# Limiting the chosen row numbers in four one-column instructions instead of one of four columns

## The chip, the cores and the metric

The kernel runs on one core of a Trainium2 chip. The metric is the time on the device in microseconds (us), as the median of a few runs. The engines are named as the profile names them: PE (TensorE's matmuls) and PEld (its weight loads), DVE (VectorE), ACT (ScalarE), POOL (GpSimd) and SP (SyncE, which issues most of the DMAs here).

## The reference, cut to what matters

```python
x = x + xattn(ctx, layernorm(x))      # x: 4 x 512 x 512, ctx: 4 x 512 x 128, "adj" is the normalized x
x = x + ffn(layernorm(x))             # 4 experts, token i goes to expert i % 4

# in each of the two attention layers, for 8 heads:
e = leaky_relu(attn_self[:, :, None] + attn_neigh[:, None, :], 0.2)
e = e + MASK_VAL * (1.0 - adj)[None, :, :]          # MASK_VAL = -1e10
alpha = softmax(e)
out = elu(alpha @ feat + b)

# in the ffn, for each expert:
inter = silu(gate) * up
out = inter @ down_proj
```

The mask is 1e10 times a normalized number, so that each row's softmax picks one row: the one at which x is largest. The attention becomes a table lookup. Row i of the attention's output is row f(f(i)) of a table y, where f(i) is the place of the largest number in row i of x. The kernel computes y for all rows, finds f, follows it twice, and adds the found row of y to x. A separate part counts in how many rows the pick is sure, and a general program is there for inputs where it isn't.

## The kernel before, in words

The four batches b have 512 rows each, laid out as 128 partitions by four tiles e (the tile is also the expert). All matmuls of the second attention layer and of the ffn are done in three terms on a high and a low part of each operand, and the low part is a subtraction on VectorE or on GpSimd, chosen by hand.

Each engine has its own list of steps, written out by hand, and the steps meet through semaphores. There are no planned times: a step runs when all before it on its engine have been issued and its semaphores have come. Of interest here:

- VectorE finds the row: `find_top(b, e)` (line 1252, the largest of each row), `find_row(b, e)` (line 1256, its place), and once per batch `rows(b)` (line 1260), which limits the places of the batch's four tiles to at most N - 1 and writes them to `f_row`. `rows(0)` to `rows(3)` stand in VectorE's list between the steps `y_value(n)` (line 1246, a tile of the table y), `h_value(b, c)` (1227), `h_low(b, c)` (1239), `r_low(r)` (1207), `turned_low(e, b)` (1286), `x2_stats` (1265), `x2_moments` (1269 and 1271) and `normalize(e, b)` (1278).
- SP stores: `store_y(n)` (line 668) puts a tile of y into the table in HBM, and `store_f(b)` (672) puts the row numbers of a batch there. Both stand in one queue with the loads of weights and inputs.
- GpSimd follows and gathers: `follow(b, e)` (line 808) fetches f(f(i)) with an indirect DMA, once `store_f(b)` has landed, and the third and fourth of a batch also wait for the first and second to have landed. `gather(b, e)` (820) adds the found rows of y to `x_sb` with an indirect DMA. Between them stand low parts, `h_low(b, c)` (801) and `r_low(r)` (795), and `x2_inverse(e, b)` (828), one over the square root of the variance.
- ScalarE makes the high parts, the exponentials and the seeds of the banks: `seed(n)` (959), `y_exp_of(n)` (965), `h_high` (950), `r_high(r)` (926), `turned_xn` (975).
- PE: `layer0`, `layer1_part` (line 1631), `turn_xn(e, b)` (1645), `first_gate` and `first_up` (1656), and then the experts (1695, 1709). Its list runs layer1_part(12, 0), layer1_part(12, 1), first_gate(0), layer1_part(12, 2) ... layer1(15), turn_xn(0, 1), first_up(0), first_gate(1), turn_xn(0, 2), first_up(1).

Of the kernel before, what the change touches and what calls it, by code (L numbers as in the profile page):

```python
# [25 lines left out]
ALU = mybir.AluOpType  # L26
# [350 lines left out]
def build(nc, x, ctx, W0, a_self0, a_neigh0, b0, W1, a_self1, a_neigh1, b1, gate_up, down, out,  # L377
          ctx_t, W0_t, W1_t, b0_t, b1_t, gate_up_t, down_t):
    B, N, D = x.shape
    F_IN = ctx.shape[2]  # L380
    H, _, FO = W0.shape
    E = gate_up.shape[0]
# [14 lines left out]
    with ExitStack() as stack:  # L397
        def sem(name):
            return stack.enter_context(nc.semaphore(name))
# [26 lines left out]
        found = sb("found", [P, B, E, 8], U32)  # L426
        f_row = sb("f_row", [P, B, E], U32)
# [127 lines left out]
        f_made = sem("f_made")  # L555
# [84 lines left out]
        def _(sp):  # L640
# [27 lines left out]
                sp.dma_start(y_rows[n // E][n % E], val[:, n % E, :]).then_inc(y_stored[n % E], 16)  # L668

            def store_f(b):  # L670
                sp.wait_ge(f_made, b + 1)
                sp.dma_start(f_rows[b], f_row[:, b, :]).then_inc(f_stored[b], 16)

            def store_out(e, b):
# [41 lines left out]
            load_r(6)  # L716
            store_y(1)
            store_f(0)
            store_y(2)
            load_r(4)  # L720
# [4 lines left out]
            store_y(4)  # L725
            store_y(5)
            store_f(1)
            store_y(6)
            store_y(7)
            store_y(8)  # L730
            store_y(9)
            store_f(2)
            store_y(10)
            store_y(11)
# [462 lines left out]
        def _(dve):  # L1197
# [59 lines left out]

            def rows(b):
                dve.wait_ge(row_found, E * (b + 1))
                nc.vector.tensor_scalar(f_row[:, b, :], found[:, b, :, 0], float(N - 1), None,  # L1260
                                        ALU.min).then_inc(f_made, 1)

            def x2_stats(e, b):
                dve.wait_ge(gathered[b][e % 2], 16 * (e // 2 + 1))
# [148 lines left out]
            find_row(0, 3)  # L1413
            y_value(1)
            rows(0)
            y_value(2)
            find_top(1, 0)
# [15 lines left out]
            h_low(2, 1)  # L1433
            h_low(2, 2)
            rows(1)
            y_value(6)
            r_low(3)
# [16 lines left out]
            find_row(2, 3)  # L1454
            h_value(3, 2)
            rows(2)
            find_row(3, 0)
            h_value(3, 3)
# [503 lines left out]
```

## Time and profile before

| | |
|---|---|
| median of 3 runs | 220.52 us (220.13 to 221.07) |
| the profiled execution | 221.49 us |
| its span in the trace | 219.7 us |
| granted clock of PE | 0.997 of full |
| PE busy | 204.8 us, 93% |
| DVE busy | 153.9 us, 70% |
| ACT busy | 103.4 us, 47% |
| POOL busy | 102.7 us, 47% |

The times in the trace count from the span's start. The profiled execution is one of many and is 0.97 us longer than the median; 1.8 us of it lie around the span. A row of the order of time has the start, the length, the engine, the line and the operation, what it writes and reads, and in brackets how long the engine was idle before it and who ended that. The length of an instruction on VectorE includes time in which it stands on the engine and can't go on. Consecutive rows on one engine overlap by some 0.08 us.

### The profile page before, as it was taken

Reading aid. Unit: us, or ns where it says so; the run is one execution under the profiler, and the core shown is the slowest. Engines: PE = TensorE matmul, PEld = TensorE weight load, DVE = VectorE, ACT = ScalarE, POOL = GpSimd, SP = SyncE. Lnnn points to the kernel's source line nnn. Section 1 sums busy time; section 2 is a strip of 40 time slices with the busy share of each in tenths; the row PEclk is TensorE's granted clock in tenths of the full one; section 3 lists DMA queues with packets and bytes.
Section 4 is the critical chain, followed back from the end, with each engine's and each line's share of the span. In section 5 each row is a group of like instructions: output and inputs, shape, how many; then the busy total and the mean of one; then the engine's idle time right before and its main releaser. Section 6 shows DMA issues by size and latency. Waiting matters only on the chain.

```text
span 219.7 us, 2706 instructions
## 1 busy us (share of the span) xinstructions
PE 204.8 (93%) x890; PEld 159.2 (72%) x890; DVE 153.9 (70%) x286; ACT 103.4 (47%) x159; POOL 102.7 (47%) x82
## 2 busy tenths in 40 slices
PE   7897899979979899999999999999999999999990
PEld 2345677856658677888888888888888888888860
DVE  0678999867999845899968947999788861510140
ACT  3799999989738332114164044653254031112100
POOL 2000968398967768898059310588035412202200
PEclk9999999999999999999999999999999999999998
DMA  6999889663622858779997365652892300140014
GB/s 203 328 428 400 230 261 349 242 107 84 125 67 64 201 128 222 111 148 160 220 373 288 107 236 162 240 224 95 296 355 117 95 2 0 55 139 0 0 69 132
DMA packets 15203, 38.80 MB, mean 177 GB/s; under 512 B 2768, under 2 KB 2768, under 8 KB 14160
## 3 DMA queue, kind: packets, MB, share of 16 engines
q1 hardware_dynamic: 12080, 34.10, 44.1%
q0 software_dynamic: 2816, 4.20, 13.6%
q10 hardware_dynamic: 288, 0.26, 0.4%
q8 instruction: 9, 0.15, 0.3%
q14 instruction: 10, 0.08, 0.1%
HBM read 30.16 MB, written 8.40 MB: 176 GB/s over the span
## 4 chain that ended last, share of the span: by engine, by line
PE 62%; DVE 17%; POOL 6%; ACT 5%; issue 4%; DMA 3%; SPq 0%; POOLq 0%; DVEq 0%
PE bank L1695 30%; PE bank L1709 15%; PE bank L1656 6%; PE bank L1682 5%; DVE hexp L1227 4%; DVE found L1256 4%; DVE val L1246 3%; DVE top L1252 3%; PE bank L1645 3%; DMA f_table<-f_row 2%; POOL ff_row L808 2%; ACT hexp L933 2%; PE bank L1739 2%; POOL x_sb L820 1%; DVE f_row L1260 1%
## 5 line engine op out<-in xcount | busy, mean ns | idle before, releaser
L1695 PE MATMUL bank<-acts,ring 128*128 128x512 f32 x288 | 67.2, 390 | 0.0
L1695 PEld LDWEIGHTS bank<-acts,ring 128*128 128x128 f32 x288 | 53.9, 188 | 11.2
L1631 PE MATMUL bank<-wide,acts 128*128 128x512 f32 x192 | 48.9, 405 | 5.3 <-ACT bank L959 2.0
L1631 PEld LDWEIGHTS bank<-wide,acts 128*128 128x128 f32 x192 | 35.4, 188 | 18.1 <-issue 5.2
L795 POOL TENSOR_TENSOR ring<-ring_raw,ring 128x1024 fp32r<-128x1024 f32 x13 | 32.6, 2518 | 31.7 <-ACT ring L926 31.7
L1709 PE MATMUL bank<-ring,wide 128*128 128x512 f32 x144 | 34.7, 392 | 0.0
L926 ACT CAST ring<-ring_raw 128x1024 fp32r<-128x1024 f32 x24 | 24.7, 1059 | 18.0 <-DMA ring_raw<-in_down_t 11.9
L1709 PEld LDWEIGHTS bank<-ring,wide 128*128 128x128 f32 x144 | 26.7, 188 | 5.4
L820 POOL DMA_INDIRECT x_sb<-y_table,ff_row x16 | 25.1, 1569 | 5.0 <-issue 4.2
L1656 PE MATMUL bank<-ring,first_xnT 128*128 128x512 f32 x96 | 23.4, 396 | 1.0 <-DVE first_xnT L1286 1.0
L1306 DVE TENSOR_TENSOR hexp<-bank,hexp 128x512 f32<-128x512 f32 x12 | 8.2, 684 | 21.0 <-PE bank L1695 21.0
L808 POOL DMA_INDIRECT ff_row<-f_table,f_row x16 | 17.2, 1077 | 9.7 <-DMA y_table<-val 4.0
L1656 PEld LDWEIGHTS bank<-ring,first_xnT 128*128 128x128 f32 x96 | 17.6, 188 | 5.0 <-DVE first_xnT L1286 1.4
L801 POOL TENSOR_TENSOR acts<-hexp,acts 128x512 fp32r<-128x512 f32 x8 | 11.4, 1510 | 19.7 <-ACT acts L950 19.7
L1011 ACT ACTIVATE hexp<-bank 128x512 f32<-128x512 f32 x12 | 7.2, 598 | 24.2 <-PE bank L1695 24.1
L1022 ACT CAST wide<-hexp 128x512 fp32r<-128x512 f32 x12 | 7.2, 622 | 22.9 <-DVE hexp L1306 22.9
L834 POOL TENSOR_TENSOR wide<-hexp,wide 128x512 fp32r<-128x512 f32 x4 | 5.2, 1289 | 26.8 <-ACT wide L1022 26.8
L1619 PE MATMUL bank<-ctxT,W_f 128*128 128x512 f32 x32 | 16.2, 630 | 0.7 <-DVE hexp L1227 0.7
L1207 DVE TENSOR_TENSOR ring<-ring_raw,ring 128x1024 fp32r<-128x1024 f32 x11 | 15.8, 1437 | 0.3 <-ACT ring L926 0.3
L1319 DVE SCALAR_TENSOR_TENSOR x_sb<-x_sb,bank 128x512 f32<-128x512 f32 x16 | 10.8, 683 | 7.2 <-PE bank L1709 5.6
L1278 DVE TENSOR_SCALAR xn<-x_sb,x2mv,rstd 128x512 f32<-128x512 f32 x16 | 12.4, 800 | 4.8 <-POOL rstd L828 4.7
L965 ACT ACTIVATE yexp<-bank,minus_one 128x512 f32<-128x512 f32 x16 | 11.0, 693 | 3.2 <-PE bank L1631 3.2
(86 smaller groups left out, 246.3 us busy)
## 6 DMA issues: line engine op xcount, KB each, us to landing
ring_raw<-in_gate_up_t SPq DMA_DIRECT2D x16, 512.0 KB, 6.1
x_sb<-in_x SPq DMA_DIRECT2D x4, 1024.0 KB, 9.7
ring_raw<-in_down_t SPq DMA_DIRECT2D x8, 512.0 KB, 6.0
y_table<-val SPq DMA_DIRECT2D x16, 256.0 KB, 3.5
out<-x_sb SPq DMA_DIRECT2D x16, 256.0 KB, 2.8
val<-in_x SPq DMA_DIRECT2D x4, 1024.0 KB
ctxT<-in_ctx_t SPq DMA_DIRECT2D x4, 256.0 KB, 5.8
wide_raw<-in_W_t SPq DMA_DIRECT2D x2, 512.0 KB, 7.6
```

The lines of the kernel that those rows point to most:

```text
L795: nc.gpsimd.tensor_tensor(ring[:, r % RING, LO, :], ring_raw[:, r % RING, LO, :], ring[:, r % RING, HI, :].bitcast(F32), ALU.subtract).the ...
L801: nc.gpsimd.tensor_tensor(hT[:, b % 2, c, LO, :], hexp[:, n % HEXP, :], hT[:, b % 2, c, HI, :].bitcast(F32), ALU.subtract).then_inc(h_lo_p ...
L808: nc.gpsimd.indirect_dma_start(out=ff_row[:, b, e:e + 1], out_offset=None, in_=f_table[b][:, :], in_offset=bass.IndirectOffsetOnAxis(ap=f_ ...
L820: nc.gpsimd.indirect_dma_start(out=x_sb[:, b, e, :], out_offset=None, in_=y_table[b][:, :], in_offset=bass.IndirectOffsetOnAxis(ap=ff_row[ ...
L926: nc.scalar.copy(ring[:, r % RING, HI, :], ring_raw[:, r % RING, LO, :]).then_inc(r_hi, 1)
L1207: nc.vector.tensor_tensor(ring[:, r % RING, LO, :], ring_raw[:, r % RING, LO, :], ring[:, r % RING, HI, :].bitcast(F32), ALU.subtract).the ...
L1278: nc.vector.tensor_scalar(xn[:, b, :], x_sb[:, b, e, :], x2mv[:, e, b, 0:1], rstd[:, e, b:b + 1], ALU.subtract, ALU.mult).then_inc(xn_made, 1)
L1619: nc.tensor.matmul(bank[Z_BANK[n]][:, :], W0_f[:, c * P:(c + 1) * P], ctxT[:, b, :], start=True, stop=True).then_inc(h_done, 1)
L1631: last = nc.tensor.matmul(bank[Y_BANK[n]][:, :], hT[:, b % 2, c, w, t * P:(t + 1) * P], W1p[:, c, v, :], start=False, stop=(c == KC - 1 an ...
L1656: last = nc.tensor.matmul(bank[(UP_BANK if half else GATE_BANK)[b]][:, :], first_xnT[:, b % 2, k, w, :], ring[:, 0:KC, v, (half * KC + k) ...
L1695: last = nc.tensor.matmul(bank[(UP_BANK if half else GATE_BANK)[KC * e + c]][:, :], ring[:, r % RING, w, col:col + P], xnT[:, (e - 1) % 2, ...
L1709: last = nc.tensor.matmul(bank[DOWN_BANK[B * e + b]][:, :], inner_parts[:, i, w, b * P:(b + 1) * P], ring[:, r % RING, v, (i % 2) * D:(i % ...
```

## The change

`rows(b)` writes its four columns with four instructions of one column each, in a loop over e, each of which raises `f_made` by one. `store_f(b)` waits for four times as high a count. Nothing else is touched: the values, the order of the lists and the transfers are the same.

```diff
             def store_f(b):
-                sp.wait_ge(f_made, b + 1)
+                sp.wait_ge(f_made, E * (b + 1))
                 sp.dma_start(f_rows[b], f_row[:, b, :]).then_inc(f_stored[b], 16)
```

```diff
             def rows(b):
                 dve.wait_ge(row_found, E * (b + 1))
-                nc.vector.tensor_scalar(f_row[:, b, :], found[:, b, :, 0], float(N - 1), None,
-                                        ALU.min).then_inc(f_made, 1)
+                for e in range(E):
+                    nc.vector.tensor_scalar(f_row[:, b, e:e + 1], found[:, b, e, 0:1], float(N - 1), None,
+                                            ALU.min).then_inc(f_made, 1)
```

## Rows read from the trace of the kernel before

**Rows 1.** The page: the span, and PE's busy time, share and instructions.

```profile
span 219.7 us, 2706 instructions
PE 204.8 (93%) x890; PEld 159.2 (72%) x890; DVE 153.9 (70%) x286; ACT 103.4 (47%) x159; POOL 102.7 (47%) x82
```

**Rows 2.** Busy time by stretches: length, each engine's us, clock, DMA share, GB/s.

```profile
60.70:82.80 22.10, 19.72 (x86) 15.41 (x86) 18.64 (x37) 11.01 (x15) 15.60 (x15) 1.00 0.49 113
82.80:214.00 131.20, 131.17 (x614) 108.65 (x614) 87.96 (x169) 39.70 (x59) 55.24 (x35) 1.00 0.51 155
```

**Rows 3.** PE in order of time, with the idle time before each.

```profile
46.09 0.97 PE L1631 MATMUL bank<-wide,acts 128*128 128x512 f32 x3 [1.23 <-POOL acts L801]
...
60.76 0.96 PE L1631 MATMUL bank<-wide,acts 128*128 128x512 f32 x3 [0.21 <-POOL acts L801]
62.71 3.02 PE L1656 MATMUL bank<-ring,first_xnT 128*128 128x512 f32 x12 [0.99 <-DVE first_xnT L1286]
...
73.14 3.02 PE L1631 MATMUL bank<-wide,acts 128*128 128x512 f32 x12 [0.61 <-ACT bank L959]
...
82.78 0.63 PE L1645 MATMUL bank<-ident,xn 128*128 128x128 f32 x4 [0.72 <-DVE xn L1278]
```

**Rows 4.** DVE in order of time: the four instructions of line 1260, and neighbours.

```profile
27.44 0.89 DVE L1260 TENSOR_SCALAR f_row<-found 128x4 uint32<-128x4 uint32 x1
...
40.62 0.16 DVE L1260 TENSOR_SCALAR f_row<-found 128x4 uint32<-128x4 uint32 x1
41.41 0.69 DVE L1246 SCALAR_TENSOR_TENSOR val<-yexp,bank 128x512 f32<-128x512 f32 x1 [0.62 <-ACT yexp L965]
...
57.65 3.09 DVE L1260 TENSOR_SCALAR f_row<-found 128x4 uint32<-128x4 uint32 x1
60.66 0.08 DVE L1256 MATCH_VALUE_LOAD found<-top,x_sb 128x8 f32 x1
...
72.38 0.42 DVE L1260 TENSOR_SCALAR f_row<-found 128x4 uint32<-128x4 uint32 x1
```

**Rows 5.** POOL in order of time, beside those four, and follow(3, 0).

```profile
25.74 3.83 POOL L801 TENSOR_TENSOR acts<-hexp,acts 128x512 fp32r<-128x512 f32 x3
...
57.61 3.09 POOL L801 TENSOR_TENSOR acts<-hexp,acts 128x512 fp32r<-128x512 f32 x2
...
71.79 1.55 POOL L820 DMA_INDIRECT x_sb<-y_table,ff_row  x1 [0.30 <-issue]
...
78.42 1.78 POOL L808 DMA_INDIRECT ff_row<-f_table,f_row  x1 [1.94 <-DMA f_table<-f_row]
```

**Rows 6.** POOL, and then DVE, in order of time from 160 to 168 us.

```profile
162.90 2.39 POOL L795 TENSOR_TENSOR ring<-ring_raw,ring 128x1024 fp32r<-128x1024 f32 x1 [9.79 <-ACT ring L926]
...
163.38 2.47 DVE L1312 TENSOR_TENSOR wide<-hexp,wide 128x512 fp32r<-128x512 f32 x1 [0.74 <-ACT wide L1022]
```

**Rows 7.** Line 1271 (ns: least, median, most); then POOL and DVE in time.

```profile
L1271 DVE TENSOR_SCALAR veps<-x2mv x16: 153/154/155, 49.5 to 113.2; 128x1 f32<-128x1 f32 x16
...
47.21 2.99 POOL L795 TENSOR_TENSOR ring<-ring_raw,ring 128x1024 fp32r<-128x1024 f32 x1
...
49.46 0.15 DVE L1271 TENSOR_SCALAR veps<-x2mv 128x1 f32<-128x1 f32 x1
```

**Rows 8.** DVE in order of time: sixteen small instructions in a row.

```profile
171.94 1.17 DVE L1349 BATCH_NORM_AGGREGATE xmv<-x2stat 128x2 f32<-128x6 f32 x16
```

**Rows 9.** The indirect DMAs of line 808, issue to landing; then the third, in time.

```profile
DMA to landing us min/median/max: 2.2/2.8/5.8
...
41.88 0.94 POOL L808 DMA_INDIRECT ff_row<-f_table,f_row  x1 [3.96 <-DMA y_table<-val]
```

**Rows 10.** DVE in order of time: h_low(3, 2).

```profile
62.58 0.67 DVE L1239 TENSOR_TENSOR acts<-hexp,acts 128x512 fp32r<-128x512 f32 x1
```

**Rows 11.** ACT in order of time: the copy for turned_low(0, 0).

```profile
58.28 0.58 ACT L975 CAST first_xnT<-bank 128x512 fp32r<-128x512 f32 x1
```

**Rows 12.** DVE in order of time: y_value(15), behind batch 3's set.

```profile
76.92 0.69 DVE L1246 SCALAR_TENSOR_TENSOR val<-yexp,bank 128x512 f32<-128x512 f32 x1 [0.64 <-ACT yexp L965]
```

**Rows 13.** The chain that ended last, in order of time: the store of batch 3.

```profile
72.86 5.30 DMA f_table<-f_row
```

## The prediction

> **What bounds the kernel now.** I read the page first, then the busy time by stretches, then the waits of the matmul engine, and last the engines around the four instructions that are changed. The span is 219.7 us and PE is busy in 93% of it [rows 1]. The stretches split that in two: from 82.8 to 214 us PE is busy for 131.17 of 131.20 us, while between 60.7 and 82.8 us it is busy for 19.72 of 22.10 us [rows 2]. So nothing that VectorE saves after 82.8 us can be seen, unless it makes PE wait; what is saved before counts only as far as it lets PE reach 82.8 us sooner. PE's idle pieces in front of that point name who holds it: 1.23 us at 46.09 for a GpSimd subtraction, 0.21 us at 60.76 for another, 0.99 us at 62.71 for VectorE's low part of the first transposed tile, 0.61 us at 73.14 for ScalarE's seed of a bank (which waited for VectorE's y_value(13)), and 0.72 us at 82.78 for VectorE's normalize(0, 2) [rows 3]. The last three all end on VectorE or on what it releases, and the wait at 82.78 is the last one of any weight before the end of the matmuls.
>
> The four instructions of line 1260 do the same work on 128x4 numbers, and took 0.89, 0.16, 3.09 and 0.42 us [rows 4]. The 0.16 us is the work. The rest is time in which the instruction stands on the engine and is held. The one of 3.09 us stands from 57.65 to 60.74 us, and GpSimd's two subtractions of line 801 stand from 57.61 to 60.70 us; the one of 0.89 us ends at 28.33 us, and three GpSimd subtractions run from 25.74 to 29.57 us, so that the second of them ends near 28.3 us; the one of 0.42 us lies in a GpSimd indirect DMA (71.79 to 73.34 us); the one of 0.16 us has none beside it [rows 4, 5]. The same holding can be seen elsewhere: a VectorE subtraction with both inputs in SBUF, of a kind that takes 0.67 us elsewhere [rows 10], stood for 2.47 us from 163.38 to 165.85 us, beside a GpSimd subtraction from 162.90 to 165.29 us [rows 6].
>
> **The change, part by part.** Removed: four instructions of four columns. Added: sixteen of one column, and the store now waits for the count of four per batch. The question is whether a one-column instruction is held as well. The nearest rows are the sixteen instructions of line 1271, the same operation on one column: 153 to 155 ns, all of them, and the one at 49.46 us lies inside a GpSimd subtraction (47.21 to 50.20 us) [rows 7]. So I take it as not held. The price of four in a row: sixteen one-instruction aggregates on two columns took 1.17 us together, that is about (1.17 - 0.15) / 15 = 0.07 us from one start to the next [rows 8]. A set of four then occupies 4 x 0.07 = 0.28 us of the engine and its last result is there 3 x 0.07 + 0.16 = 0.37 us after its start. The bounds for a set are 0.28 us and 4 x 0.16 = 0.64 us (each waits for the end of the one before).
>
> [...]
>
> *Batch 0* (27.44 us). 0.89 us less the 0.08 us of overlap with the next start is 0.81 us; it becomes 0.28 us: VectorE is 0.53 us ahead from there. VectorE has no idle until 41.41 us, where it waits 0.62 us for ScalarE [rows 4], so the gain on VectorE itself ends there. It can only pass on through the transfers: y_value(3) releases a store on the SP queue, and behind it stand three loads. GpSimd's first indirect DMA lands 5.8 us after its issue (median 2.8 us), and the third, which needs that landing, starts at 41.88 us after 3.96 us of idle [rows 9]; behind it in GpSimd's order stands the subtraction for which PE waits 1.23 us. If the loads are what delays it, up to 0.53 us reaches PE; if not, nothing. I take the middle, 0.27 us.
>
> *Batch 1* (40.62 us). 0.16 us becomes 0.28 us of engine and 0.37 us to the last result: 0.12 to 0.2 us more, in front of the idle 0.62 us at 41.41 [rows 4]. It costs nothing as long as that idle is longer. The store of the row numbers goes 0.2 us later; its reader on GpSimd, follow(1, 0), stands behind r_low(4), which ends at 50.20 us [rows 7].
>
> *Batch 2* (57.65 us). The next instruction starts at 60.66 us; in the new kernel it can start at 57.93 us, which is 2.73 us sooner [rows 4]. From there three instructions (find_row(3, 0), h_value(3, 3), turned_low(0, 0)) take 62.58 - 60.66 = 1.92 us and come to 59.85 us [rows 4, 10]. Their inputs are there: ScalarE's copy for turned_low(0, 0) was done at 58.86 us [rows 11], and its part of h_value(3, 3) stands ahead of that in its list. The fourth, h_low(3, 2), reads two SBUF tiles, and GpSimd's second subtraction still runs until 60.70 us [rows 5]; by the holding of [rows 6] it is held until then. So it begins at 60.70 instead of 62.58 us: 1.88 us of the 2.73 us survive, 0.85 us are given back to the same hold. PE's wait of 0.99 us at 62.71 us goes (turned_low is done at 59.9 us, before PE is free at 61.72 us). Now all of VectorE's work up to rows(3) follows without a wait of its own, so line 1260 of batch 3 starts at 72.38 - 1.88 = 70.50 us, and PE's wait of 0.61 us at 73.14 us goes too, since seed(15) is then ready at about 71.2 us and PE only comes there at 73.14 - 0.61 - 0.99 = 71.54 us. PE is then 1.60 us ahead.
>
> *Batch 3* (72.38 us). The last result was there at 72.80 us, and comes now at 70.50 + 0.37 = 70.87 us, 1.93 us sooner. The two VectorE instructions behind it move 0.21 us back, in front of an idle of 0.64 us at 76.92 us [rows 12]; no cost. The store of the row numbers took 5.30 us to land, behind the 256 KB of store_y(13) on the same queue [rows 13]; both move together, so I keep the 5.30 us. The landing releases follow(3, 0) on GpSimd (78.42 us) [rows 5], follow(3, 1), the inverse of batch 2's tile, normalize(0, 2), and PE's turn_xn(0, 2) at 82.78 us. That chain moves by 1.93 us to 80.85 us. PE by its own path would be there at 82.78 - 0.72 - 1.60 = 80.46 us, so it still waits, 0.4 us, and the chain through f_table sets the gain: 1.93 us.
>
> **The sum.** 1.93 + 0.27 = 2.20 us, with bounds of 1.5 us (batch 0 gives nothing, normalize(0, 1) is held by an indirect DMA for the 0.26 us that batch 3's instruction stood over its 0.16 us, and a set costs 0.64 us) and 2.5 us. After 82.8 us PE has no idle, so the whole shift reaches the end. The profiled execution took 221.49 us (219.7 us of span and 1.8 us around it) and would take 219.3 us; the median of the three runs is 0.97 us under that execution, so the forecast for the median is 220.52 - 2.20 = 218.3 us, between 218.0 and 219.0 us.
>
> **Rivals.**
> *The chain through f_table does not move* (0.17). All that PE gains before 82.78 us is lost if normalize(0, 2) isn't earlier: PE would then simply wait 0.72 + 1.60 = 2.3 us there. That is so where the 5.30 us landing is bound by other transfers (the gathers of batch 2, in the same microseconds) and not by the store in front of it, or where GpSimd comes late to follow(3, 0). For it: the 5.30 us is long for 2 KB. Against it: the gathers themselves wait for VectorE's y_value(11) and so move too. It gives 0 to 1 us, 219.5 to 220.5 us; I take 220.1 us.
> *The change doesn't do what it can do: one column is held like four* (0.06). Each set's first instruction is then held to the same moment and three more follow: 3 x 0.07 = 0.21 us later in batches 2 and 3, 220.7 us. [...] Against it stand the 153 to 155 ns of line 1271 beside GpSimd work [rows 7].
> *Each of the four asks anew and loses each time* (0.04, the slower side). In batch 0 the second would be held to the end of GpSimd's third subtraction, 29.57 us, 1.3 us more; in batch 2 the other three meet the indirect DMAs that come next on GpSimd, at the 0.26 us by which batch 3's instruction stood over its 0.16 us, 0.8 us. With half of batch 0 reaching PE it makes 0.65 + 0.8 = about 1.5 us, 222.0 us. It decides from the point where a one-column instruction beside GpSimd work takes more than its 0.16 us.
> *Something not costed on the way* (0.04 slower by over 0.5%, 0.03 same): VectorE and GpSimd meet at other moments, and a GpSimd subtraction held by VectorE (h_low(3, 1), awaited by PE at 60.76 us) costs 0.6 us a time. Two such at the wrong place and a later gather undo the gain.
>
> **How the numbers follow.** The forecast has 0.66 of the chance (218.0 to 219.0 us and somewhat beyond), the first rival 0.17. A difference of 0.5%, 1.1 us, is about what a measurement of this kernel can tell from no change. Faster by over that means under 219.42 us: 0.66 from the forecast and 0.05 of the first rival, 0.71. Within it: 0.12 of the first rival, 0.06 of the second and 0.03 of the last, 0.21. Slower: 0.04 of the third and 0.04 of the last, 0.08. The range that holds 8 in 10 runs from 217.5 us (batch 0 in full, plus half a microsecond of runs) to 220.5 us (the first rival's far end).
>
> **What would show it.** In the new trace the sixteen instructions of the line should each take about 0.16 us; h_low(3, 2) on VectorE should stand for over a microsecond and end with GpSimd's subtraction; PE's waits of 0.99 and 0.61 us should be gone and the one before turn_xn(0, 2) should be about 0.4 us, at about 80.8 us or slightly sooner; PE should have no idle behind it. The prediction is wrong if a one-column instruction stands for longer than 0.2 us, or if the landing of f_table in batch 3 doesn't come about 2 us sooner.

## The result and the profile after

| | before | after |
|---|---|---|
| median of 20 runs each | 220.44 us (219.52 to 221.76) | 219.25 us (217.57 to 220.42) |
| the profiled execution | 221.49 us | 219.58 us |
| its span | 219.7 us | 217.7 us |
| granted clock of PE | 0.997 | 0.983 |

The ratio is 0.9943 with a 95% interval from 0.9924 to 0.9962: the changed kernel is 1.26 us faster (0.84 to 1.68 us; the ratio is one of means, the medians differ by 1.19 us). Two more measurements of the same kernel gave 0.9955 and 0.9912. The forecast was 2.20 us of gain and 218.3 us. The sign and the wide range (217.5 to 220.5 us) hold. The bounds of the sum itself, 1.5 to 2.5 us of gain and 218.0 to 219.0 us, do not: the gain is a good half of what was expected. In the profiled execution the span is 2.0 us shorter, and 0.57 us of that is there before any changed instruction: PE's 30 matmuls near 23 us start at 22.98 us, and at 23.55 us in the kernel before.

The lines of VectorE, in order of time (start, length, engine, line, operation, and in brackets the idle before it with who ended it), answer to [rows 4] and [rows 10]. Line 1261 is what line 1260 was, and later lines are one up.

```profile
26.86 0.33 DVE L1261 TENSOR_SCALAR f_row<-found 128x1 uint32<-128x1 uint32 x4
...
39.55 0.33 DVE L1261 TENSOR_SCALAR f_row<-found 128x1 uint32<-128x1 uint32 x4
40.83 0.69 DVE L1246 SCALAR_TENSOR_TENSOR val<-yexp,bank 128x512 f32<-128x512 f32 x1 [0.95 <-ACT yexp L965]
41.43 1.22 DVE L1207 TENSOR_TENSOR ring<-ring_raw,ring 128x1024 fp32r<-128x1024 f32 x1
...
58.25 0.32 DVE L1261 TENSOR_SCALAR f_row<-found 128x1 uint32<-128x1 uint32 x4
58.49 0.08 DVE L1256 MATCH_VALUE_LOAD found<-top,x_sb 128x8 f32 x1
...
60.41 1.49 DVE L1239 TENSOR_TENSOR acts<-hexp,acts 128x512 fp32r<-128x512 f32 x1
61.82 0.68 DVE L1246 SCALAR_TENSOR_TENSOR val<-yexp,bank 128x512 f32<-128x512 f32 x1
...
71.03 0.33 DVE L1261 TENSOR_SCALAR f_row<-found 128x1 uint32<-128x1 uint32 x4
```

The set of batch 2 stands for 0.32 us, although GpSimd is at work beside it as before (58.22 to 61.34 us, below), and the next instruction starts 0.24 us after the set's start. GpSimd is at work beside three of the four sets; beside that of batch 1 (39.55 us) it is idle. The summary of the line has all sixteen, in ns (least, median, most):

```profile
L1261 DVE TENSOR_SCALAR f_row<-found x16: 138/144/151, 26.9 to 71.2; 128x1 uint32<-128x1 uint32 x16
```

GpSimd in order of time, to be read with [rows 5] and [rows 9]:

```profile
34.81 1.29 POOL L808 DMA_INDIRECT ff_row<-f_table,f_row  x1 [0.19 <-issue]
36.41 1.53 POOL L808 DMA_INDIRECT ff_row<-f_table,f_row  x1 [0.30 <-issue]
41.68 1.79 POOL L808 DMA_INDIRECT ff_row<-f_table,f_row  x1 [3.74 <-DMA y_table<-val]
43.77 1.60 POOL L820 DMA_INDIRECT x_sb<-y_table,ff_row  x1 [0.30 <-DMA y_table<-val]
44.80 1.87 POOL L801 TENSOR_TENSOR acts<-hexp,acts 128x512 fp32r<-128x512 f32 x1
...
58.22 3.12 POOL L801 TENSOR_TENSOR acts<-hexp,acts 128x512 fp32r<-128x512 f32 x2
...
76.49 0.99 POOL L808 DMA_INDIRECT ff_row<-f_table,f_row  x1 [1.13 <-DMA f_table<-f_row]
```

The third indirect DMA took 1.79 us, where it took 0.94 us before [rows 9], and the one after it, gather(0, 0), starts at 43.77 us. Its start is the marker that I use below. The profile names a store of y as what ended the wait ahead of both, but by the kernel's list the third indirect DMA waits for the landing of the first one and of store_f(0), and not for a store of y. In the kernel before, the row of gather(0, 0), and ahead of it that of r_low(3) on VectorE, were

```profile
42.01 1.22 DVE L1207 TENSOR_TENSOR ring<-ring_raw,ring 128x1024 fp32r<-128x1024 f32 x1
...
43.12 1.60 POOL L820 DMA_INDIRECT x_sb<-y_table,ff_row  x1 [0.30 <-issue]
```

PE in order of time, to be read with [rows 3]:

```profile
46.73 1.65 PE L1632 MATMUL bank<-wide,acts 128*128 128x512 f32 x3 [2.44 <-POOL acts L801]
48.17 1.88 PE L1620 MATMUL bank<-ctxT,W_f 128*128 128x512 f32 x2
...
58.31 4.38 PE L1632 MATMUL bank<-wide,acts 128*128 128x512 f32 x18
62.53 2.88 PE L1657 MATMUL bank<-ring,first_xnT 128*128 128x512 f32 x12
65.25 9.69 PE L1632 MATMUL bank<-wide,acts 128*128 128x512 f32 x42
74.77 0.60 PE L1646 MATMUL bank<-ident,xn 128*128 128x128 f32 x4
75.12 5.72 PE L1657 MATMUL bank<-ring,first_xnT 128*128 128x512 f32 x24
80.69 0.60 PE L1646 MATMUL bank<-ident,xn 128*128 128x128 f32 x4
```

The waits of [rows 3] from 60 us on are all gone: PE runs from 58.31 us on without one, and comes to turn_xn(0, 2) at 80.69 us instead of 82.78 us. But the wait near 46 us has doubled, from 1.23 to 2.44 us, and the three matmuls behind it took 1.65 us where they took 0.97 us [rows 3]. Of the 1.21 us that the wait has grown, 0.57 us are PE's earlier start, and 0.64 us are a later end, at 46.73 us and not at 46.09 us. The stretches (length, then busy us of PE, PEld, DVE, ACT and POOL, the granted clock, the DMAs' share, GB/s) show why the matmuls are slower:

```profile
44.00:46.00 2.00, 0.28 (x2) 0.00 (x0) 1.77 (x4) 1.76 (x3) 2.00 (x2) 1.00 0.33 122
46.00:47.00 1.00, 0.27 (x1) 0.28 (x2) 0.00 (x0) 0.00 (x0) 0.84 (x2) 0.74 0.50 62
47.00:48.00 1.00, 1.00 (x3) 0.81 (x4) 0.00 (x0) 0.00 (x0) 1.00 (x2) 0.50 0.84 150
```

After 2.44 us without a matmul PE's granted clock is 0.50 of full, and it is back at 1.00 from 50 us on. So in these two profiles the waits around batch 2 are gone, and something around batch 0 went the other way. The experiments try to take the two apart.

### The profile page after: what moved, and what is told of

It is laid out like the page before. It is cut to its first block, busy times and chain, and to the rows that moved or that the text cites. A ratio compares the mean times of both kernels' runs of the same rounds, so it can differ in the third digit from the quotient of the medians.

```text
span 217.7 us, 2718 instructions
## 1 busy us (share of the span) xinstructions
PE 204.2 (94%) x890; PEld 160.1 (74%) x890; DVE 151.1 (69%) x298; ACT 103.3 (47%) x159; POOL 102.7 (47%) x82
## 4 chain that ended last, share of the span: by engine, by line
PE 78%; DVE 8%; ACT 7%; POOL 2%; issue 1%; DMA 1%; ACTq 0%; POOLq 0%
PE bank L1696 30%; PE bank L1710 15%; PE bank L1657 10%; PE bank L1632 10%; PE bank L1683 5%; PE bank L1646 3%; PE bank L1620 2%; ACT hexp L933 2%; DVE found L1256 2%; DVE hexp L1227 2%; DVE top L1252 2%; DVE val L1246 2%; PE bank L1740 2%; ACT hexp L939 1%; DMA y_table<-val 1%
## 5 line engine op out<-in xcount | busy, mean ns | idle before, releaser
L1632 PEld LDWEIGHTS bank<-wide,acts 128*128 128x128 f32 x192 | 36.2, 191 | 17.6 <-issue 5.0
L808 POOL DMA_INDIRECT ff_row<-f_table,f_row x16 | 18.0, 1124 | 9.6 <-DMA y_table<-val 3.7
L1022 ACT CAST wide<-hexp 128x512 fp32r<-128x512 f32 x12 | 7.2, 621 | 22.4 <-DVE hexp L1307 22.4
```

Of the source, the lines that this page charges most:

```text
L808: nc.gpsimd.indirect_dma_start(out=ff_row[:, b, e:e + 1], out_offset=None, in_=f_table[b][:, :], in_offset=bass.IndirectOffsetOnAxis(ap=f_ ...
L1632: last = nc.tensor.matmul(bank[Y_BANK[n]][:, :], hT[:, b % 2, c, w, t * P:(t + 1) * P], W1p[:, c, v, :], start=False, stop=(c == KC - 1 an ...
```

## Experiments

The theory: the time comes from batch 2 alone, by the hold that a one-column instruction escapes, and batch 0 has a cost of its own. The rivals: batch 0 helps too; the number of columns doesn't matter but their being odd does; the whole is a matter of how the execution starts. Ratios are to the kernel before, measured beside each group on the same chip.

**The change once more** (no edit).

> The changed kernel once more, beside the kernel before on one chip. Theory (the hold): each one-column instruction takes 0.15 us, the sets 0.33 us, and PE has no idle between 58 and 81 us; ratio about 0.994, as in the 20 runs. Rival (the gain is a matter of the start of the execution, since the first matmuls of the changed kernel's trace came 0.58 us earlier than those of the kernel before, ahead of any changed instruction): the ratio lies within 0.3% of 1. The trace also tells whether the fall of PE's clock near 46 us, for 3.4 us, which the changed kernel's profile shows and that of the kernel before doesn't, comes again.

Measured: 219.89 us, ratio 0.9955 (0.9925 to 0.9985); the profile repeats the one above: sets of 0.33 us, PE's wait of 2.44 us before 46.87 us with the clock at 0.50 behind it (47 to 50 us), no wait past 58 us. A later measurement, with the expectation

> The changed kernel once more, for the comparison on this chip with the three others. Expected at about 0.995 of the kernel before, with a mean granted clock of 0.988 or less in about half of the executions (15 of 32 so far), against 3 of 56 of the kernel before.

gave 219.24 us and 0.9912 (0.9876 to 0.9949), and 2 of its 8 executions had a low clock. The rival that it is only the start falls: three measurements, 40 executions in all, have their intervals under 1. The start does matter in a single profile. Over all profiles here PE's 30 matmuls near 23 us start anywhere from 22.4 to 23.6 us, ahead of any changed instruction, and in the changed kernel that offset goes through to the end: from there to the end of the span it takes 194.6 to 194.8 us in its three profiles, and 196.1 us in the kernel before, 1.4 us more (the table further down has them all).

**Only batch 2 split.** The edit, shortened; store_f(b) waits for the counts that fit, here and in the next two.

```diff
-                for e in range(E):
-                    ...
+                if b in (2,):
+                    ... four of one column
+                else:
+                    ... one of four columns
```

> Only rows(2) is split, the sets of batches 0, 1 and 3 stay one instruction of four columns. Theory (all of the gain is the hold of 3.09 us in batch 2): as fast as the full change, or faster by up to 1 us if the earlier start of batch 0's followers brings an unfavourable meeting at 36 to 44 us; VectorE's instruction of batch 0 stands for about 0.9 us again. Ratio 0.987 to 0.994. Rival (the gain comes from batch 0 as well, by the 0.53 us that VectorE is ahead): slower than the full change by about 0.5 us.

Measured: 219.61 us, ratio 0.9948 (0.9921 to 0.9975), as fast as the full change. Its trace, DVE, POOL and PE in order of time (its lines are shifted; 1266 is the instruction of four columns, 1263 the set of one, 809 and 821 the indirect DMAs):

```profile
27.43 0.90 DVE L1266 TENSOR_SCALAR f_row<-found 128x4 uint32<-128x4 uint32 x1
57.63 0.32 DVE L1263 TENSOR_SCALAR f_row<-found 128x1 uint32<-128x1 uint32 x4
...
41.47 0.94 POOL L809 DMA_INDIRECT ff_row<-f_table,f_row  x1 [3.56 <-DMA ff_row<-f_table,f_row]
42.72 1.98 POOL L821 DMA_INDIRECT x_sb<-y_table,ff_row  x1 [0.30 <-issue]
...
46.06 0.97 PE L1637 MATMUL bank<-wide,acts 128*128 128x512 f32 x3 [1.21 <-POOL acts L802]
```

With batch 0 left alone the third indirect DMA takes 0.94 us, gather(0, 0) starts at 42.72 us, and PE waits 1.21 us as in the kernel before. The rival that batch 0 helps by 0.5 us has nothing for it here. But the times don't show a cost of batch 0 either: without one this kernel should be faster than the full change beside it, and 0.9948 and 0.9955 can't be told apart. Its gain of 1.15 us (0.55 to 1.74 us) also falls short of the 1.93 us forecast for batch 2, although batch 0 is left alone.

**All but batch 2 split** (`if b in (0, 1, 3)`).

> rows(0), rows(1) and rows(3) are split, rows(2) stays one instruction of four columns. Theory: batch 2's instruction stands for about 3.1 us beside GpSimd's two subtractions of line 801, PE waits about 1 us for the first transposed tile and 0.6 us for seed(15), and the gain is gone: 219.9 to 221.5 us, the upper end if splitting batch 0 costs something by itself. Rival (a gain in batch 0): 219.9 us or less, 0.5 us under the kernel before.

Measured: 221.24 us, ratio 1.0028 (1.0004 to 1.0053): slower than the kernel before. Batch 2's instruction stands for 3.09 us again, and the waits at 62.80 and 73.23 us are back (DVE and PE in order of time):

```profile
57.74 3.09 DVE L1266 TENSOR_SCALAR f_row<-found 128x4 uint32<-128x4 uint32 x1
...
46.17 0.97 PE L1637 MATMUL bank<-wide,acts 128*128 128x512 f32 x3 [2.44 <-POOL acts L802]
62.80 3.02 PE L1662 MATMUL bank<-ring,first_xnT 128*128 128x512 f32 x12 [0.99 <-DVE first_xnT L1292]
73.23 3.03 PE L1637 MATMUL bank<-wide,acts 128*128 128x512 f32 x12 [0.62 <-ACT bank L960]
```

PE's wait of 2.44 us before 46.17 us is no loss by itself. It ends 0.08 us later than in the kernel before, and is longer because PE's matmuls near 23 us started 1.13 us sooner in this execution, at 22.42 us. So the gain is batch 2's: with it split the time is 0.5% under the kernel before, without it the other three sets together cost up to 0.5%. Which of the three costs it, the time doesn't tell. Beside each other, the full change and this kernel differ by 1.35 us (219.89 against 221.24 us).

**Three columns and one.** Each set becomes two instructions.

```diff
-                for e in range(E):
-                    nc.vector.tensor_scalar(f_row[:, b, e:e + 1], ...).then_inc(f_made, 1)
+                for lo, hi in ((0, 3), (3, 4)):
+                    nc.vector.tensor_scalar(f_row[:, b, lo:hi], ...).then_inc(f_made, 1)
```

> Each set is two instructions, of three columns and of one. It tells whether it is the odd number of columns or the single column that keeps an instruction from being held. If an odd number is enough, both take about 0.15 us in batch 2 and the time is that of the full change, about 0.99 of the kernel before. [...] I expect the second, at 0.7.

Measured: 220.55 us, ratio 1.0024 (0.9997 to 1.0052). The line's summary in ns, and the set of batch 2 in order of time:

```profile
L1261 DVE TENSOR_SCALAR f_row<-found x8: 136/254/3087, 26.6 to 71.8; 128x3 uint32<-128x3 uint32 x4, 128x1 uint32<-128x1 uint32 x4
...
56.95 3.14 DVE L1261 TENSOR_SCALAR f_row<-found 128x3 uint32<-128x3 uint32 x2
```

Three columns are held like four (3.09 us), and all of the gain is gone. That the number is odd is not enough. It is the single column that is not held: the sixteen of the changed kernel took 138 to 151 ns, twelve of them beside work on GpSimd. I had expected three columns to be held, at 0.7, and the time of the kernel before with it, 220 to 221 us.

**The load of batch 3's x, later.** In batch 0 GpSimd waits for its first indirect DMA to land. I had left open whether the loads under way set that landing. The test moves a load of 1 MB behind it.

```diff
             load_ctx(3)
-            load_x(3)
             store_y(4)
             store_y(5)
+            load_x(3)
             store_f(1)
```

> The changed kernel with the load of batch 3's x (1 MB) moved on the SP queue from behind load_ctx(3) to behind store_y(5), some 6 us later. Theory (the landing of GpSimd's first indirect DMA near 41 us is set by the loads that are under way, so that time gained on VectorE in batch 0 can't pass): that landing comes 1 us or more sooner, PE's wait of 2.4 us near 46.7 us shrinks to under 1.2 us, PE's clock no longer falls there, and the time is 1 to 2.5 us below that of the changed kernel. Rival (the landing is slow by itself, or the third indirect DMA waits for something else): PE's wait stays at 2 us and more, and the time is that of the changed kernel within 0.3%.

> The kernel before with the same move of the load of batch 3's x. Theory: PE's wait of 1.2 us near 46 us goes, but the hold of 3.1 us in batch 2 stays (both move sooner together), so that it gains 0.5 to 1.2 us on the kernel before and stays 1.5 to 2 us behind the changed kernel with the same move. Rival (PE's path after 57 us is set by VectorE's hold alone): no gain, ratio within 0.3% of 1.

Measured: 217.13 us, ratio 0.9827 (0.9791 to 0.9862) with the change; a second measurement gave 217.20 us and 0.9826, with the expectation

> The changed kernel with the later load of batch 3's x, again, for a narrower interval and beside the next: 0.983 of the kernel before, 217.1 us, no execution with a clock of 0.988 or less.

and the kernel before with the same move took 219.27 us, ratio 0.9922 (0.9892 to 0.9952). GpSimd of the changed kernel with the later load, in order of time; and, from the chain that ended last, the landing of its first indirect DMA:

```profile
40.35 0.94 POOL L808 DMA_INDIRECT ff_row<-f_table,f_row  x1 [1.81 <-DMA ff_row<-f_table,f_row]
41.60 1.61 POOL L820 DMA_INDIRECT x_sb<-y_table,ff_row  x1 [0.30 <-issue]
...
35.41 4.20 DMA ff_row<-f_table,f_row
```

The landing now is at 39.6 us instead of 41.0 to 41.9 us (in four profiles with batch 0 split and the load in its old place), gather(0, 0) starts at 41.60 us, and PE has no wait between 23.6 and 57.7 us, where the next one (1.16 us) begins. No execution in the five measurements of kernels with the later load had a mean clock of 0.988 or less (0 of 36; the changed kernel 17 of 40, the kernel before 6 of 77). This load holds up the landing; that was the theory's side. The kernel before gained more from the move than I had allowed (1.7 us for 0.5 to 1.2 us).

The two kernels with the later load also measure the change where PE has no wait near 46 us in either: 219.27 against 217.13 us, 2.1 us.

**The meeting at 41.7 us.** In the changed kernel's profile r_low(3) (line 1207) starts 0.25 us ahead of the third indirect DMA, in the kernel before 0.13 us behind it. The test moves r_low(3) behind find_top(2, 0).

```diff
             y_value(6)
-            r_low(3)
             find_top(2, 0)
+            r_low(3)
             y_value(7)
```

> The changed kernel with r_low(3) and find_top(2, 0) exchanged on VectorE. In the changed kernel r_low(3) (both inputs in SBUF) starts 0.2 us ahead of GpSimd's third indirect DMA near 41.7 us, which then stood for 1.55 to 1.79 us in place of 0.94 us; in the kernel before the DMA started 0.13 us ahead of it. Theory (the loss in batch 0 comes from this meeting): the DMA takes about 0.95 us again, gather(0, 0) starts 0.6 to 0.8 us sooner, and the time is 0.3 to 0.8 us below the changed kernel's, more if PE's clock then doesn't fall. Rival (a wait for a store holds the gather, not the DMA in front of it): gather(0, 0) starts where it did, near 43.8 us, and the time is unchanged.

> The changed kernel with both: the load of batch 3's x later and r_low(3) behind find_top(2, 0). If the two losses are separate, the best of the four: 1.5 to 3 us below the changed kernel, 217 to 218 us. If the earlier landing already parts the indirect DMA from r_low(3), it is the same as with the later load alone.

Measured: 219.45 us, ratio 0.9939 (0.9914 to 0.9964), and 217.61 us, ratio 0.9848 (0.9812 to 0.9884). The trace of the first (DVE and POOL in order of time):

```profile
42.69 1.21 DVE L1207 TENSOR_TENSOR ring<-ring_raw,ring 128x1024 fp32r<-128x1024 f32 x1
...
42.60 0.94 POOL L808 DMA_INDIRECT ff_row<-f_table,f_row  x1 [4.01 <-DMA y_table<-val]
43.84 1.61 POOL L820 DMA_INDIRECT x_sb<-y_table,ff_row  x1 [0.30 <-issue]
```

The DMA takes 0.94 us again, so the meeting is real. It also answers the rival that the gather waits for a store of y, as the profile of the changed kernel has it: here the gather starts 1.64 us after y_value(6)'s store was issued (at 42.20 us), and in the changed kernel that store took 2.25 us to land. But in this execution the landing of the first indirect DMA came 0.9 us later (41.9 us), so that the gather starts where it did, and the time doesn't tell this kernel from the changed one. What the meeting costs in the median stays open; the expected 0.3 to 0.8 us weren't seen, and on top of the later load the exchange brought nothing.

**PE kept at work through the wait.** keep_on(12) is twelve small matmuls into a bank that is no longer needed.

```diff
-            layer1(8)
-            pe.wait_ge(h_made, 11)
+            layer1_part(8, 0)
+            layer1_part(8, 1)
+            layer1_part(8, 2)
+            pe.wait_ge(h_made, 11)
+            keep_on(12)
+            layer1_part(8, 3)
```

> The changed kernel with twelve small matmuls (128x128 by 128x256, about 0.1 us each, into a bank whose content is no longer needed) ahead of layer1_part(8, 3), where PE waits 2.4 us near 46.7 us for GpSimd's low part. They take nothing away and only fill 1.3 us of that idle. [...]

Measured: 219.29 us, ratio 0.9922 (0.9889 to 0.9955), against 219.24 us for the changed kernel beside it. PE in order of time:

```profile
44.73 1.48 PE L1734 MATMUL bank<-ident,ones_bf 128*128 128x256 bf16 x12
47.35 0.96 PE L1632 MATMUL bank<-wide,acts 128*128 128x512 f32 x3 [1.14 <-POOL acts L801]
60.89 0.94 PE L1632 MATMUL bank<-wide,acts 128*128 128x512 f32 x3 [0.45 <-POOL acts L801]
```

The clock never falls (0 of 12 executions at 0.988 or less, and three matmuls take 0.96 us again), as expected, and nothing is gained. One of the twelve took 422.44 us; it is not in the ratio, and nothing here shows why. I had expected the time 0.5 to 1 us below that of the changed kernel, about 0.991 of the kernel before, by the clock alone. That was wrong: PE, now faster from 47 to 58 us, waits 0.45 us before 60.89 us for GpSimd's low part. The kernel before had the same wait, a row that the prediction left out:

```profile
59.62 0.94 PE L1631 MATMUL bank<-wide,acts 128*128 128x512 f32 x3 [0.43 <-POOL acts L801]
```

GpSimd's order from gather(0, 0) to that low part sets the time, and the slower clock spent slack. Over the 40 executions of the changed kernel those with a low clock took 219.87 us on average and the others 218.98 us; by this experiment something that comes with the fall, such as a longer wait, is a likelier cause of the difference than the clock; it was not shown. What brings the fall isn't settled either: 5 of 12 executions of only batch 2, whose profiled one waits 1.21 us, 6 of 12 of all but batch 2 and 7 of 12 with the exchange of r_low(3) had a low clock too. For only batch 2 the split of batch 0 can't be what brings it.

**GpSimd's order.** h_low(3, 0) ahead of gather(1, 1), on top of the later load.

> The same, with h_low(3, 0) put ahead of gather(1, 1) on GpSimd. With the later load PE's longest wait past 25 us is 1.2 us at 58.9 us, for h_low(3, 0), which stands behind gather(1, 1) on GpSimd although its input is there. If that wait is what bounds PE now: 0.5 to 1 us less, 216.3 us. If PE is held next by what the gather's later issue delays (normalize(0, 1) doesn't read it, x2_stats(1, 1) does, far later), or h_low(3, 1) only moves behind the gather: no change, 217.1 us.

Measured: 217.21 us, ratio 0.9825 (0.9784 to 0.9865), no change. PE's wait only moved to the second low part, which now stands behind the gather, and grew:

```profile
59.87 0.96 PE L1632 MATMUL bank<-wide,acts 128*128 128x512 f32 x3 [1.47 <-POOL acts L801]
```

## Why the prediction was right in its sign and too large

*The hold.* Right. One-column instructions took 138 to 151 ns beside GpSimd's work, the sets 0.32 to 0.33 us (0.37 forecast) and 0.24 us of the engine in batch 2 (0.28). One more instruction costs the engine less than its own length of 138 to 151 ns: a set of four takes 0.24 us of it.

*What is given back.* Right. h_low(3, 2) stood for 1.49 us, from 60.41 to 61.90 us, and GpSimd's second subtraction was done at 61.34 us: it was held until there and then did its work. I had written that it would end with GpSimd's subtraction; it ended 0.56 us behind it. From the start of batch 2's set to the start of the instruction behind h_low(3, 2) it took 5.52 us before (57.65 to 63.17 us) and now 3.57 us (58.25 to 61.82 us), 1.95 us less against the 1.88 us of the forecast.

*The sum for batch 2.* About right in size, and in part by luck. Starts and spans in the profiled executions:

| kernel | PE's 30 matmuls us | r_low(3) us | third indirect DMA us (its length) | gather(0, 0) us | span us | from the gather to the end |
|---|---|---|---|---|---|---|
| before | 23.55 | 42.01 | 41.88 (0.94) | 43.12 | 219.7 | 176.6 |
| all but batch 2 | 22.42 | 40.88 | 41.75 (1.16) | 43.21 | 218.8 | 175.6 |
| three and one | 22.68 | 41.13 | 41.17 (0.94) | 42.41 | 218.3 | 175.9 |
| only batch 2 | 23.54 | 42.00 | 41.47 (0.94) | 42.72 | 217.0 | 174.3 |
| the change | 22.98 | 41.43 | 41.68 (1.79) | 43.77 | 217.7 | 173.9 |
| the change, again | 23.13 | 41.58 | 42.06 (1.55) | 43.91 | 217.9 | 174.0 |
| the change, a third time | 22.99 | 41.46 | 41.93 (1.57) | 43.81 | 217.6 | 173.8 |
| with the exchange of r_low(3) | 23.61 | 42.69 | 42.60 (0.94) | 43.84 | 217.7 | 173.9 |
| kept busy | 23.58 | 42.05 | 42.70 (1.39) | 44.39 | 218.2 | 173.8 |

From gather(0, 0) to the end it is 173.8 to 174.3 us where batch 2's set is split, and 175.6 to 176.6 us where it is not: 1.3 to 2.8 us, around the 1.93 us of the forecast. The times give 1.15 us (only batch 2 against the kernel before), 1.35 us (the full change against all but batch 2) and 2.1 us (with the later load). The 0.4 us of idle that I left at turn_xn(0, 2) was not there, since follow(3, 0) started at 76.49 us, 1.93 us sooner than at 78.42 us [rows 5], and then took 0.99 us in place of 1.78 us; so PE and not the f_table chain came last. That 1.93 us is the forecast's number, but not its sum: the store of batch 3 was issued only 1.35 us sooner (71.51 and 72.86 us), and landed in 4.7 us, where I had kept 5.30 us.

*The step that failed: batch 0.* I took 0.27 us of gain, midway between nothing and 0.53 us. No run shows a gain: only batch 2 is as fast as the full change, and all but batch 2 is slower than the kernel before (ratio 1.0028, which is for three sets together). The step of the prediction that failed is the one by which VectorE's half microsecond could pass on through the transfers. GpSimd's first indirect DMA lands at 41.2 us in the kernel before and between 41.0 and 41.9 us in four profiled executions in which batch 0 is split, no sooner for VectorE being ahead; with the 1 MB load moved behind it, it lands at 39.6 us.

Counted from PE's 30 matmuls, which takes the start of the execution out, the table shows more. r_low(3) comes 18.45 to 18.47 us behind them in every kernel but the one with the exchange, so the change doesn't bring it forward: VectorE's lead goes into its wait at 40.83 us, as the prediction had it for VectorE itself. What moves is the third indirect DMA, which waits for the landing: 17.93 to 18.49 us behind the matmuls where batch 0 is left whole (three profiles), and 18.70 to 19.33 us where it is split (six). So it comes behind r_low(3), and wherever it does so by 0.25 us or more it ends 0.81 to 0.82 us after r_low(3) ends, however late it started. That puts gather(0, 0) 20.8 us behind the matmuls in all five such profiles, against 19.2 to 19.7 us in the three. Why the landing comes later with batch 0 split no run shows. This meeting was not in the prediction; nor was the one of the second indirect DMA with r_low(2), for which VectorE's lead does count (1.53 us at 36.41 us in place of 0.94 us) and behind which no wait shows.

The markers above put gather(0, 0) 0.65 to 0.8 us later in the three profiled executions of the change, which is about what is missing: 1.93 - 0.7 = 1.2 us, against 1.26 us measured. The match proves little. It is a sum of single executions, the exchange of r_low(3) did not give the 0.7 us back, and only batch 2, which has no such delay in its profile, gained no more than the full change (1.15 us). So no run shows a gain from batch 0; that it costs something is likely from the profiles and from all but batch 2; and what takes the rest of the forecast's 2.20 us stays open.

*The rivals.* That the chain through f_table doesn't move: no, it moved by 1.93 us. That one column is held like four: no, but three are. That each of four asks anew: no. The meetings of VectorE and GpSimd and a later gather stood under "something not costed", at 0.07, as something that brings no gain or a loss. A gain of half the size was not among the cases; the range held it only because it was drawn for the others, which is luck, as is that 219.25 us lies just under the 219.42 us that I had set for faster.

## What to carry to other kernels

Where a short instruction stands for microseconds (here 3.09 us for 0.16 us of work), look at what the neighbour engine does in the same microseconds, and try a shape that isn't held: here one column at a time, sixteen instructions for four, each of 138 to 151 ns. Then follow the engine that is now early through the next meetings and landings: VectorE's lead from batch 0 went into its next wait (0.95 us in place of 0.62 us), and an instruction of VectorE that came first held the neighbour in turn (1.79 us in place of 0.94 us). The larger gain lay in the queue: a 1 MB load issued 6 to 8 us later was worth 2.0 us on top of the change (217.2 against 219.2 us), and the two together are 1.7% faster than the kernel before.

## What the runs showed of the hardware that I had not expected

- The limiting instruction was held beside GpSimd's two subtractions with three columns as with four (3.09 us each); with one column it was not (138 to 151 ns, all sixteen, twelve of them beside GpSimd's work).
- The hold outlasted the GpSimd instruction that it began with. At 57.65 us it went through the end of an indirect DMA (56.60 to 58.15 us) and two subtractions (3.09 us), and again in all but batch 2 and in three and one, while in batch 0 it ended near the boundary of two subtractions (0.89 us) [rows 4, 5].
- A subtraction on VectorE, r_low(3), held a GpSimd indirect DMA that started 0.25 us after it: 1.79 us in place of 0.94 us. In five profiles the DMA started 0.25 to 0.87 us behind and ended 0.81 to 0.82 us after the subtraction; at 0.04 us behind, in three and one, it took 0.94 us. With r_low(3) moved behind it the DMA took 0.94 us again.
- After 2.44 us without a matmul PE's granted clock went to 0.50 for 3.4 us in the profiled executions of the changed kernel, and not after the 1.23 us of the kernel before; after 2.44 us in the one with all but batch 2 split it stayed at 1.00. Keeping the clock up there gained nothing that could be measured (219.29 against 219.24 us).
